# The second layer norm of a gated cross-attention and FFN block: its apply step moved from VectorE to ScalarE

## The chip, the cores and the metric

One core of one Trainium2 chip runs the kernel. The metric is the device time of one execution in microseconds (us). Three runs of the kernel before took 345.74 us in the median (345.51 to 346.2).

## What is computed

```python
# x, ctx: [32, 128, 256]; D = 256; B = 32 sequences, S = 128 positions
x = x + tanh(g_xattn) * mix(layernorm(x), ctx)     # mix: a recurrence over the 128 positions
x = x + tanh(g_ffn)   * ffn(layernorm(x))
# mix, for every position t:
#   r     = decay * r + ctx_t * ctx_t
#   inp   = (ln_t * r) @ Wi.T + bi
#   gate  = sigmoid(inp @ Wg.T + bg)
#   state = tanh((gate * state + (1 - gate) * inp) @ A.T + inp @ Bm.T)
#   out_t = state @ Wo.T + bo
# ffn: relu(ln @ Q(W1).T + b1) @ Q(W2) + b2, with Q a ternary quantisation; F = 1024 hidden units
# layernorm: (x - mean) / sqrt(var + 1e-5), over the last axis, without weights
```

The second layer norm, of x after the attention, is the one that the change concerns.

## The kernel before

The 128 positions are cut into 16 chunks of T = 8 positions. A chunk of x is a tile of 128 partitions by TILES = 2 by 256 values; transposed data has K = 2 blocks of 128 features by N = 256 columns (8 positions of 32 sequences). Products that need more than one pass are written as sums of a high and a low part.

The program is a software pipeline over 18 bodies (`run`, L191 to L198; four are written out at either end and the rest is a loop of two). Body c works on five chunks at once (`stages`, L200): **norm** on chunk c+2, **project** on c+1, **chain** on c, **attend** on c-1 and **ffn** on c-2. So bodies 1 to 16 have an attend stage, bodies 0 to 14 a project stage, bodies 0 to 13 a norm stage, and bodies 0 to 15 a chain stage. Each body has eight slots j = 0 to 7, one for each position of the chain's chunk, and each engine has its own queue, written out by hand slot by slot. An engine does its instructions in that order; semaphores tie the engines together.

The recurrence is the backbone of each slot: VectorE forms m_hi, m_all and m_lo from the last state and the gate (`gated_state`, L573 to L591), TensorE multiplies them (`step`, L840 to L854), ScalarE takes the tanh (`tanh_step`, L427 to L431). Around it stand, in the part of the body that the change touches:

- TensorE: slot 4 `gate_product` (L823), slot 5 the step, three y products and `x1_t` (L868), which transposes xh2 into att_ps; slot 6 the step, two y products and `from_inp(…, 0)` (L828); slot 7 the step, `from_inp(…, 1)` and `from_rest` (L834), which waits for rest_lo.
- ScalarE: slot 5 the tanh, `gate_out` (L390 to L395, two sigmoids of 128x256) and `square` (L365); slot 6 the tanh, `rest_high` (L397) and `normed_high` (L406), the high part of the transposed xh2.
- VectorE: slot 3 `x1_stats` and `x1_mean` (L607, L614) of chunk c-1; slot 5 the gated state, `x1_apply` (L619 to L624) and a hidden low part; slot 6 the gated state, `rest_all` (L561, which waits for the gate), and `scan` (L528 to L541: two small cx instructions and the scan of r for chunk c+2); slot 7 the gated state, `rest_low`, `normed_low` and `finish`.
- GpSimd: once a body, after mean2, the variance plus epsilon (L334) and its power -0.5 (L336) on 128x2 values, then a wait for xh2_set and two accumulating DMAs, of b2_g into x1 (L340) and of bo_g into x_res (L348). The first must not overtake the reading of x1, so it waits until xh2 is written. `finish` (L638) needs b2_added one body later, and `residual` (L599) bo_added in slot 2 of the next body.

Before the bodies and in bodies 0 and 1 TensorE is fed with products of an idle tile (`keep_warm`, L910) wherever it would stand still. All of ScalarE's functions in the bodies (Tanh, Sigmoid, Identity, Relu, Square, copies) run after one table load at the start.

Of the kernel before, what the change touches and what calls it, by code (L numbers as in the profile page):

```python
# [18 lines left out]
def build(nc, x_in, ctx_in, wsq_in, w1_in, w2_in, cols_in, rows_in, out):  # L19
# [33 lines left out]
    with ctx:  # L53
        def sb(name, shape, dt=f32):
            return ctx.enter_context(nc.sbuf_tensor(name, shape, dt))
# [60 lines left out]
        x1 = sb("x1", [P, 2, TILES, D])  # L116
        st2, mv2 = sb("st2", [P, TILES, 6]), sb("mv2", [P, TILES, 2])
        ve2, rs2 = sb("ve2", [P, TILES]), sb("rs2", [P, TILES])
        xh2 = sb("xh2", [P, TILES, D])
        xt_hi = sb("xt_hi", [P, 2, K, N], f16)  # L120
        xt_lo = sb("xt_lo", [P, 2, K, N], f16)
# [38 lines left out]
        bo_added = [sem("bo_added0"), sem("bo_added1")]  # L160
        b2_added = [sem("b2_added0"), sem("b2_added1")]
        stats2, mean2, vare2, rstd2, xh2_set = (sem(n) for n in ("stats2", "mean2", "vare2", "rstd2", "xh2_set"))
        xh2_t, xt_hi_set, xt_lo_set = sem("xh2_t"), sem("xt_hi_set"), sem("xt_lo_set")
        hid_sum, hid_set, h_hi_set, h_lo_set = sem("hid_sum"), sem("hid_set"), sem("h_hi_set"), sem("h_lo_set")
        y_sum, y_set = sem("y_sum"), sem("y_set")
# [112 lines left out]
        def _(pool):  # L278
            nc.gpsimd.memset(idle[:, :], 0.0).then_inc(idle_set, 1)
            nc.gpsimd.memset(ident[:, :], 0.0).then_inc(const_set, 1)  # L280
            nc.gpsimd.memset(ones[:, :], 1.0).then_inc(const_set, 1)
            nc.gpsimd.memset(minus_half[:, :], -0.5)
            nc.gpsimd.memset(eps[:, :], LN_EPS).then_inc(const_set, 1)
            nc.gpsimd.memset(state[:, 1, :, N - B:N], 0.0).then_inc(const_set, 1)
            pool.wait_ge(const_set, 4)
# [34 lines left out]
            def body(c):  # L320
                norm, project, chain, attend, ffn = stages(c)
                if norm:
                    rstd1_of(norm)
                if isinstance(c[0], int) and c[1] == 0:
                    low("wo", wo_scaled, wo_hi, wo_lo)
                    find_below(0, 6)
                if isinstance(c[0], int) and c[1] == 1:
                    find_below(6, 8)
                if attend:

                    if chain:
                        pool.wait_ge(x_res_in[chain[1] % 2], landed(chain))
                    pool.wait_ge(mean2, upto(attend))
                    nc.gpsimd.tensor_tensor(ve2[:, :], mv2[:, :, 1], eps[:, :], ALU.add).then_inc(vare2, 1)  # L334
                    pool.wait_ge(vare2, upto(attend))
                    nc.gpsimd.tensor_tensor(rs2[:, :], ve2[:, :], minus_half[:, :], ALU.pow).then_inc(rstd2, 1)  # L336

                    pool.wait_ge(const_set, 5)
                    pool.wait_ge(xh2_set, upto(attend))
                    pool.dma_start(x1[:, attend[1] % 2, :, :], b2_g[:, :].unsqueeze(1).to_broadcast([P, TILES, D]),  # L340
                                   accum_op=ALU.add).then_inc(b2_added[attend[1] % 2], 16)
                if chain:

                    if isinstance(c[0], int) and c[1] == 0:
                        pool.wait_ge(dve_prep, done["gates_out"])
                    if not attend:
                        pool.wait_ge(x_res_in[chain[1] % 2], landed(chain))
                    pool.dma_start(x_res[:, chain[1] % 2, :, :], bo_g[:, :].unsqueeze(1).to_broadcast([P, TILES, D]),  # L348
                                   accum_op=ALU.add).then_inc(bo_added[chain[1] % 2], 16)
# [4 lines left out]
        def _(act):  # L354
# [53 lines left out]
                nc.scalar.mul(xt_hi[:, q[1] % 2, :, :], att_ps[:, :].rearrange("p (k n) -> p k n", k=K), NORM_SCALE).then_inc(xt_hi_set, 1)  # L408


            def hidden(q, p):
                act.wait_ge(hid_sum, upto(q, PAIRS, p + 1))

                if p >= 2:
                    act.wait_ge(h_lo_set, upto(q, PAIRS, p - 1))
                elif exists(plus(q, -1)):
                    act.wait_ge(h_lo_set, upto(plus(q, -1), PAIRS, PAIRS + p - 1))
                for u in range(2):
                    last = nc.scalar.activation(hid[:, p % 2, u, :], hid_ps[p % 2][:, u * N:(u + 1) * N], ACT.Relu,  # L419
                                                bias=b1_s[:, 2 * p + u:2 * p + u + 1])  # L420
                last.then_inc(hid_set, 1)
# [37 lines left out]
            def body(c):  # L459
# [4 lines left out]
                for j in range(T):  # L464
# [7 lines left out]
                    if j == 3 and project:  # L472
                        inp_out(project)
                    if j == 5:
                        if project:
                            gate_out(project)
                        if norm:
                            square(norm)
# [22 lines left out]
        def _(dve):  # L501
# [114 lines left out]
                    last = nc.vector.bn_aggr(mv2[:, t, :], st2[:, t, :])  # L616
                last.then_inc(mean2, 1)

            def x1_apply(q):  # L619
                dve.wait_ge(rstd2, upto(q))  # L620
                for t in range(TILES):
                    last = nc.vector.tensor_scalar(xh2[:, t, :], x1[:, q[1] % 2, t, :], mv2[:, t, 0:1], rs2[:, t:t + 1],  # L622
                                                   ALU.subtract, ALU.mult)
                last.then_inc(xh2_set, 1)  # L624

            def normed_low(q):
                dve.wait_ge(xt_hi_set, upto(q))
                nc.vector.scalar_tensor_tensor(out=xt_lo[:, q[1] % 2, :, :], in0=att_ps[:, :].rearrange("p (k n) -> p k n", k=K),  # L628
# [102 lines left out]
            def body(c):  # L731
                norm, project, chain, attend, ffn = stages(c)
                peeled = c[1] if isinstance(c[0], int) else None
                for j in range(T):
# [31 lines left out]
                        if ffn:  # L766
                            hidden_low(ffn, 2)
                    if j == 5:
                        if attend:
                            x1_apply(attend)  # L770
                        if ffn:
                            hidden_low(ffn, 3)
                    if j == 6:
# [251 lines left out]
```

## Time and profile before

| | |
|---|---|
| median of three runs | 345.74 us |
| the profiled execution's own time | 345.45 us |
| its span, first to last instruction | 343.7 us |
| TensorE busy | 318.0 us (93%) |
| VectorE busy | 294.7 us (86%) |
| ScalarE busy | 217.0 us (63%) |
| GpSimd busy | 90.8 us (26%) |
| one body, bodies 2 to 13 | 18.47 us |
| mean granted TensorE clock | 0.985 |

The busy times include overlap of an instruction's tail with the next one's start: an instruction's length in a view is from its start to its end, and the next on the same engine can start about 0.1 us before that end. Where the next start is known, the distance of two starts is what an instruction costs its queue. Body c of bodies 2 to 13 begins at about 65.5 + 18.47 (c - 2) us of the span; the body shown in the rows is body 8 (176.8 to 195.3 us). A chain of waits is followed back from the last instruction: it lists, in order of time, the pieces of work of which each released the next.

### The profile page before, as it was taken

The page shows a single profiled execution, that of the slowest core. Times are in us where ns is not written, and L with a number is a line of the kernel's source. Part 1 is how long each engine was busy: PE and PEld are TensorE (multiplying, and loading weights), DVE is VectorE, ACT ScalarE, POOL GpSimd, SP SyncE. Part 2 cuts the span into 40 slices and gives each one's busy share as a digit, 9 for nine tenths or more (in the row PEclk, how much of TensorE's full clock was granted, in tenths as well). Part 3 has the DMA queues.
Part 4 walks back from the last instruction along what each step waited for, and adds up shares of the span by engine and source line. Part 5 has one row for each costly group of instructions (what it writes and reads, how often), then busy time and mean ns, then how long its engine had stood idle before and what let it go on. Part 6 is the DMA issues. An engine that isn't in the chain of part 4 may idle for free.

```text
span 343.7 us, 10093 instructions
## 1 busy us (share of the span) xinstructions
PE 318.0 (93%) x3805; PEld 285.9 (83%) x3805; DVE 294.7 (86%) x868; ACT 217.0 (63%) x501; POOL 90.8 (26%) x119
## 2 busy tenths in 40 slices
PE   8778697899999999999999999999999999999985
PEld 5667586798989898989898998989898989897764
DVE  5885888789989898989898989989898989877653
ACT  3546342486767767675849586766767575847653
POOL 4413951222131312213122222131312212121220
PEclk9989988999999999999999999999999999999999
DMA  7920221614424251716152433324161515150520
GB/s 273 367 96 2 62 32 31 124 33 62 125 42 115 50 137 32 153 31 133 50 94 89 61 122 57 123 34 122 38 145 31 92 31 93 32 93 2 93 62 31
DMA packets 19239, 29.16 MB, mean 85 GB/s; under 512 B 1808, under 2 KB 10000, under 8 KB 18960
## 3 DMA queue, kind: packets, MB, share of 16 engines
q0 software_dynamic: 8704, 8.39, 17.3%
q1 hardware_dynamic: 10080, 19.93, 17.0%
q10 hardware_dynamic: 432, 0.53, 0.5%
q8 instruction: 15, 0.25, 0.3%
q14 instruction: 8, 0.07, 0.1%
HBM read 16.26 MB, written 4.19 MB: 60 GB/s over the span
## 4 chain that ended last, share of the span: by engine, by line
PE 73%; ACT 10%; DVE 10%; issue 3%; POOL 0%; DVEq 0%
PE pre_ps L804 14%; PE hid_ps L890 12%; PE y_ps L902 11%; PE ret_ps L804 8%; PE pre_ps L845 7%; PE inp_ps L804 7%; PE att_ps L863 6%; PE pre_ps L851 4%; ACT inp L384 3%; DVE inp_lo L558 3%; ACT inp_hi L388 3%; PE att_ps L872 2%; PE ret_ps L815 2%; ACT state L429 2%; PE hid_ps L912 1%
## 5 line engine op out<-in xcount | busy, mean ns | idle before, releaser
L429 ACT ACTIVATE state<-pre_ps,sc 128x64 f32<-128x64 f32 x128 | 40.0, 312 | 90.6 <-PE pre_ps L851 90.6
L419 ACT ACTIVATE hid<-hid_ps,b_s 128x256 f32<-128x256 f32 x128 | 53.5, 470 | 13.5 <-PE hid_ps L890 11.8
L890 PE MATMUL hid_ps<-xt_hi,w_q 128*128 128x256 f16 x256 | 59.1, 272 | 1.2 <-DVE xt_lo L628 0.8
L902 PE MATMUL y_ps<-w_q,h_hi 128*128 128x256 bf16 x256 | 59.3, 273 | 0.3 <-DVE h_lo L635 0.3
L890 PE MATMUL hid_ps<-xt_lo,w_q 128*128 128x256 f16 x256 | 59.1, 272 | 0.0
L902 PE MATMUL y_ps<-w_q,h_lo 128*128 128x256 bf16 x256 | 59.1, 272 | 0.0
L635 DVE TENSOR_TENSOR h_lo<-hid,h_hi 128x512 f16<-128x512 f32 x64 | 44.0, 687 | 8.2 <-ACT h_hi L425 6.7
L845 PE MATMUL pre_ps<-m_hi,a_hi 128*128 128x32 f16 x512 | 42.9, 178 | 4.1 <-DVE m_hi L586 3.9
L845 PEld LDWEIGHTS pre_ps<-m_hi,a_hi 128*128 128x128 f16 x512 | 35.1, 96 | 11.0 <-DVE m_hi L586 8.8
L845 PE MATMUL pre_ps<-m_hi,a_lo 128*128 128x32 f16 x512 | 41.8, 176 | 0.0
L425 ACT CAST h_hi<-hid 128x512 f16<-128x512 f32 x64 | 39.6, 619 | 2.0
L586 DVE SCALAR_TENSOR_TENSOR m_hi<-state,gate 128x64 f16<-128x64 f32 x128 | 27.4, 214 | 10.8 <-ACT state L429 10.4
L340 POOL DMA_DIRECT2D x<-b_g x16 | 19.8, 1238 | 56.9 <-DVE xh L622 56.9
L851 PE MATMUL pre_ps<-m_lo,a_hi 128*128 128x32 f16 x512 | 32.5, 177 | 0.6
L845 PEld LDWEIGHTS pre_ps<-m_hi,a_lo 128*128 128x128 f16 x512 | 32.1, 96 | 0.9
L591 DVE TENSOR_TENSOR m_lo<-m_all,m_hi 128x64 f16<-128x64 f32 x128 | 28.8, 225 | 4.4
L334 POOL TENSOR_TENSOR ve<-mv,eps 128x2 f32<-128x2 f32 x16 | 4.5, 282 | 93.7 <-DVE mv L616 93.7
L804 PE MATMUL ret_ps<-inp_hi,wg_hi 128*128 128x256 f32 x64 | 20.1, 314 | 9.1 <-DVE inp_lo L558 9.1
L890 PEld LDWEIGHTS hid_ps<-xt_hi,w_q 128*128 128x128 bf16 x256 | 24.8, 97 | 4.4 <-DVE xt_lo L628 1.1
L902 PEld LDWEIGHTS y_ps<-w_q,h_hi 128*128 128x128 f16 x256 | 24.8, 97 | 4.1 <-DVE h_lo L635 1.0
L588 DVE SCALAR_TENSOR_TENSOR m_all<-state,gate 128x64 f32<-128x64 f32 x128 | 27.8, 217 | 0.0
L902 PEld LDWEIGHTS y_ps<-w_q,h_lo 128*128 128x128 f16 x256 | 25.0, 98 | 2.4
(131 smaller groups left out, 929.1 us busy)
## 6 DMA issues: line engine op xcount, KB each, us to landing
x_norm<-x_in SPq DMA_DIRECT2D x16, 256.0 KB, 2.8
cx<-ctx_in SPq DMA_DIRECT2D x16, 256.0 KB, 3.1
x_res<-x_in SPq DMA_DIRECT2D x16, 256.0 KB, 2.6
x_res<-bo_g POOLq DMA_DIRECT2D x16, 256.0 KB, 4.8
x<-b_g POOLq DMA_DIRECT2D x16, 256.0 KB, 3.9
y_out<-y SPq DMA_DIRECT2D x16, 256.0 KB, 2.0
w_raw<-w_in SPq DMA_DIRECT2D x2, 1024.0 KB, 9.0
wsq<-wsq_in SPq DMA_DIRECT2D x3, 256.0 KB, 6.3
```

Source lines behind the costliest of these rows:

```text
L419: last = nc.scalar.activation(hid[:, p % 2, u, :], hid_ps[p % 2][:, u * N:(u + 1) * N], ACT.Relu, bias=b1_s[:, 2 * p + u:2 * p + u + 1])
L425: nc.scalar.copy(h_hi[:, 2 * p:2 * p + 2, :], hid[:, p % 2, :, :]).then_inc(h_hi_set, 1)
L429: nc.scalar.activation(state[:, q[1] % 2, :, step_cols(j)], pre_ps[q[1] % 2][:, :].rearrange("p (k n) -> p k n", k=K)[:, :, step_cols(j)], ...
L586: nc.vector.scalar_tensor_tensor(out=m_hi[:, :, :], in0=before, scalar=STATE_SCALE, in1=now, op0=ALU.mult, op1=ALU.mult).then_inc(m_hi_set, 1)
L588: nc.vector.scalar_tensor_tensor(out=m_all[:, :, :], in0=before, scalar=STATE_SCALE, in1=now, op0=ALU.mult, op1=ALU.mult).then_inc(m_all_s ...
L591: nc.vector.tensor_tensor(m_lo[:, :, :], m_all[:, :, :], m_hi[:, :, :], ALU.subtract).then_inc(m_lo_set, 1)
L635: nc.vector.tensor_tensor(h_lo[:, 2 * p:2 * p + 2, :], hid[:, p % 2, :, :], h_hi[:, 2 * p:2 * p + 2, :], ALU.subtract).then_inc(h_lo_set, 1)
L804: last = nc.tensor.matmul(out_of(m), w[:, k, cut], v[:, k, :], start=start and n == 0 and (m == 0 or stop), stop=stop and n == len(terms) - 1,
L845: nc.tensor.matmul(pre_ps[q[1] % 2][:, m * N + j * B:m * N + (j + 1) * B], w[:, k, m * P:(m + 1) * P], m_hi[:, k, :], start=False, stop=Fa ...
L851: last = nc.tensor.matmul(pre_ps[q[1] % 2][:, m * N + j * B:m * N + (j + 1) * B], a_hi[:, k, m * P:(m + 1) * P], m_lo[:, k, :], start=Fals ...
L890: last = nc.tensor.matmul(hid_ps[p % 2][:, u * N:(u + 1) * N], w1_q[:, k, cut], v[:, par, k, :], start=n == 0, stop=n == len(terms) - 1)
L902: last = nc.tensor.matmul(y_ps[:, t * D:(t + 1) * D], h[:, f, t * P:(t + 1) * P], w2_q[:, f, :], start=f == 0 and t == 0 and h is h_hi, st ...
```

## The change

Two ScalarE activations, Identity with scale = rs2 and bias = shift2 (both columns of one value per partition), take the place of VectorE's two tensor_scalar instructions. They stand in slot 5 between the tanh and the gate. GpSimd makes the bias, shift2 = -mean2 * rs2, in two instructions more for each chunk, with one semaphore more (scaled2), and a constant of -1 is set once.

```diff
--- before.py
+++ after.py
@@ -116,6 +116,8 @@
         x1 = sb("x1", [P, 2, TILES, D])
         st2, mv2 = sb("st2", [P, TILES, 6]), sb("mv2", [P, TILES, 2])
         ve2, rs2 = sb("ve2", [P, TILES]), sb("rs2", [P, TILES])
+        off2, shift2 = sb("off2", [P, TILES]), sb("shift2", [P, TILES])
+        minus_one = sb("minus_one", [P, TILES])
         xh2 = sb("xh2", [P, TILES, D])
         xt_hi = sb("xt_hi", [P, 2, K, N], f16)
         xt_lo = sb("xt_lo", [P, 2, K, N], f16)
@@ -160,6 +162,7 @@
         bo_added = [sem("bo_added0"), sem("bo_added1")]
         b2_added = [sem("b2_added0"), sem("b2_added1")]
         stats2, mean2, vare2, rstd2, xh2_set = (sem(n) for n in ("stats2", "mean2", "vare2", "rstd2", "xh2_set"))
+        scaled2 = sem("scaled2")
         xh2_t, xt_hi_set, xt_lo_set = sem("xh2_t"), sem("xt_hi_set"), sem("xt_lo_set")
         hid_sum, hid_set, h_hi_set, h_lo_set = sem("hid_sum"), sem("hid_set"), sem("h_hi_set"), sem("h_lo_set")
         y_sum, y_set = sem("y_sum"), sem("y_set")
@@ -280,6 +283,7 @@
             nc.gpsimd.memset(ident[:, :], 0.0).then_inc(const_set, 1)
             nc.gpsimd.memset(ones[:, :], 1.0).then_inc(const_set, 1)
             nc.gpsimd.memset(minus_half[:, :], -0.5)
+            nc.gpsimd.memset(minus_one[:, :], -1.0)
             nc.gpsimd.memset(eps[:, :], LN_EPS).then_inc(const_set, 1)
             nc.gpsimd.memset(state[:, 1, :, N - B:N], 0.0).then_inc(const_set, 1)
             pool.wait_ge(const_set, 4)
@@ -331,9 +335,12 @@
                     if chain:
                         pool.wait_ge(x_res_in[chain[1] % 2], landed(chain))
                     pool.wait_ge(mean2, upto(attend))
-                    nc.gpsimd.tensor_tensor(ve2[:, :], mv2[:, :, 1], eps[:, :], ALU.add).then_inc(vare2, 1)
+                    nc.gpsimd.tensor_tensor(ve2[:, :], mv2[:, :, 1], eps[:, :], ALU.add)
+                    nc.gpsimd.tensor_tensor(off2[:, :], mv2[:, :, 0], minus_one[:, :], ALU.mult).then_inc(vare2, 1)
                     pool.wait_ge(vare2, upto(attend))
-                    nc.gpsimd.tensor_tensor(rs2[:, :], ve2[:, :], minus_half[:, :], ALU.pow).then_inc(rstd2, 1)
+                    nc.gpsimd.tensor_tensor(rs2[:, :], ve2[:, :], minus_half[:, :], ALU.pow).then_inc(scaled2, 1)
+                    pool.wait_ge(scaled2, upto(attend))
+                    nc.gpsimd.tensor_tensor(shift2[:, :], off2[:, :], rs2[:, :], ALU.mult).then_inc(rstd2, 1)
 
                     pool.wait_ge(const_set, 5)
                     pool.wait_ge(xh2_set, upto(attend))
@@ -407,6 +414,13 @@
                 act.wait_ge(xh2_t, upto(q))
                 nc.scalar.mul(xt_hi[:, q[1] % 2, :, :], att_ps[:, :].rearrange("p (k n) -> p k n", k=K), NORM_SCALE).then_inc(xt_hi_set, 1)
 
+
+            def x1_apply(q):
+                act.wait_ge(rstd2, upto(q))
+                for t in range(TILES):
+                    last = nc.scalar.activation(xh2[:, t, :], x1[:, q[1] % 2, t, :], ACT.Identity,
+                                                bias=shift2[:, t:t + 1], scale=rs2[:, t:t + 1])
+                last.then_inc(xh2_set, 1)
 
             def hidden(q, p):
                 act.wait_ge(hid_sum, upto(q, PAIRS, p + 1))
@@ -472,6 +486,8 @@
                     if j == 3 and project:
                         inp_out(project)
                     if j == 5:
+                        if attend:
+                            x1_apply(attend)
                         if project:
                             gate_out(project)
                         if norm:
@@ -615,13 +631,6 @@
                 for t in range(TILES):
                     last = nc.vector.bn_aggr(mv2[:, t, :], st2[:, t, :])
                 last.then_inc(mean2, 1)
-
-            def x1_apply(q):
-                dve.wait_ge(rstd2, upto(q))
-                for t in range(TILES):
-                    last = nc.vector.tensor_scalar(xh2[:, t, :], x1[:, q[1] % 2, t, :], mv2[:, t, 0:1], rs2[:, t:t + 1],
-                                                   ALU.subtract, ALU.mult)
-                last.then_inc(xh2_set, 1)
 
             def normed_low(q):
                 dve.wait_ge(xt_hi_set, upto(q))
@@ -766,8 +775,6 @@
                         if ffn:
                             hidden_low(ffn, 2)
                     if j == 5:
-                        if attend:
-                            x1_apply(attend)
                         if ffn:
                             hidden_low(ffn, 3)
                     if j == 6:
```

## Rows read from the trace of the kernel before

**Rows 1.** Busy time, share and instructions of each engine, from the page
```profile
PE 318.0 (93%) x3805; PEld 285.9 (83%) x3805; DVE 294.7 (86%) x868; ACT 217.0 (63%) x501; POOL 90.8 (26%) x119
```

**Rows 2.** By stretch: length, busy us of PE, PEld, DVE, ACT, POOL; granted clock, DMA
```profile
47.00:65.50 18.50, 15.65 (x182) 13.27 (x182) 14.01 (x42) 7.43 (x19) 8.07 (x8) 0.89 0.30 49
176.80:195.30 18.50, 18.01 (x229) 16.65 (x230) 17.27 (x53) 12.79 (x30) 4.30 (x6) 1.00 0.37 85
324.00:343.70 19.70, 14.69 (x124) 11.30 (x122) 9.47 (x18) 10.49 (x22) 2.51 (x3) 1.00 0.17 41
```

**Rows 3.** TensorE in order of time, steady body (start, length, engine, line, tiles)
```profile
188.57 0.39 PE L804 MATMUL ret_ps<-inp_hi,wg_hi 128*128 128x256 f32 x1 [0.46 <-DVE inp_lo L558]
...
192.16 0.60 PE L872 MATMUL att_ps<-ident,xh 128*128 128x128 f32 x4
...
194.25 0.28 PE L804 MATMUL pre_ps<-inp_lo,bm_hi 128*128 128x256 f32 x1
194.37 0.28 PE L804 MATMUL pre_ps<-inp_hi,bm_lo 128*128 128x256 f32 x1
194.62 0.19 PE L845 MATMUL pre_ps<-m_hi,a_hi 128*128 128x32 f16 x1
```

**Rows 4.** VectorE in order of time, the same body
```profile
191.85 0.22 DVE L591 TENSOR_TENSOR m_lo<-m_all,m_hi 128x64 f16<-128x64 f32 x1
192.12 0.69 DVE L563 SCALAR_TENSOR_TENSOR rest<-gate,inp 128x512 f32<-128x512 f32 x1
...
193.22 1.22 DVE L538 TENSOR_TENSOR_SCAN r<-keep,cx 128x512 f32<-128x512 f32 x1
194.36 0.20 DVE L586 SCALAR_TENSOR_TENSOR m_hi<-state,gate 128x64 f16<-128x64 f32 x1
```

**Rows 5.** ScalarE in order of time, the same body
```profile
191.04 0.31 ACT L429 ACTIVATE state<-pre_ps,sc 128x64 f32<-128x64 f32 x1 [1.20 <-PE pre_ps L851]
191.25 0.83 ACT L393 ACTIVATE gate<-ret_ps,cols 128x256 f32<-128x256 f32 x2
191.97 0.64 ACT L369 ACTIVATE cx<-cx 128x512 f32<-128x512 f32 x1
```

**Rows 6.** The chain of waits in body 1, up to the last step product
```profile
61.44 0.84 ACT gate L393 x2
...
62.30 0.69 DVE rest L563
...
63.41 1.22 DVE r L538
```

**Rows 7.** Groups of ScalarE instructions by line and shape: busy us, mean ns
```profile
L393 ACT ACTIVATE gate<-ret_ps,cols 128x256 f32<-128x256 f32 x32 | 13.3, 471 | 1.4 <-PE ret_ps L804 1.4
...
L404 ACT ACTIVATE s_hi<-state 128x512 f16<-128x512 f32 x16 | 10.1, 630 | 0.8
...
L408 ACT ACTIVATE xt_hi<-att_ps 128x512 f16<-128x512 f32 x16 | 9.6, 597 | 1.5 <-PE att_ps L872 1.5
...
L444 ACT ACTIVATE bm_hi<-wsq,sc 128x512 fp32r<-128x512 f32 x1 | 0.7, 718 | 0.0
```

**Rows 8.** VectorE in order of time, body 14
```profile
304.35 0.22 DVE L586 SCALAR_TENSOR_TENSOR m_hi<-state,gate 128x64 f16<-128x64 f32 x1 [0.62 <-ACT state L429]
```

**Rows 9.** ScalarE in order of time, slot 5 of body 15
```profile
317.64 0.31 ACT L429 ACTIVATE state<-pre_ps,sc 128x64 f32<-128x64 f32 x1
```

**Rows 10.** TensorE in order of time, body 15
```profile
318.48 0.60 PE L872 MATMUL att_ps<-ident,xh 128*128 128x128 f32 x4
```

**Rows 11.** The chain of waits in body 16
```profile
327.48 0.56 POOL ve L334
...
328.10 0.72 POOL rs L336
...
328.85 0.75 DVE xh L622 x2
```

**Rows 12.** GpSimd in order of time, the steady body
```profile
192.30 1.69 POOL L348 DMA_DIRECT2D x_res<-bo_g  x1
```

## The prediction

> **What bounds the kernel now.** I read the page's busy times first. TensorE is busy for 93% of the span, VectorE for 86%, ScalarE for 63% [rows 1]. In a steady body the same holds more sharply: of 18.50 us TensorE is busy for 18.01 and VectorE for 17.27, at a granted clock of 1.00 [rows 2]. By these shares alone an instruction taken from VectorE and given to ScalarE looks like a gain. So the second reading is of one body in order of time, and the question is what TensorE waits for. It waits in two places. Ahead of the gate product it stands still for 0.46 us for inp_lo [rows 3], which hangs on the tanh of slot 3 and lies before the edit. And ahead of the step of slot 7: the last two products of from_inp start at 194.25 and 194.37, 0.12 apart, and the step at 194.62, 0.25 later [rows 3]. So TensorE loses about 0.13 us there, and m_hi of slot 7 (L586) is written at 194.36 + 0.20 = 194.56, just before it starts [rows 4].
>
> Now what puts m_hi there: the third reading, backwards along VectorE and ScalarE. The rest (L563) starts at 192.12, the scan at 193.22 (with the cx pair between them), m_hi at 194.36, each right behind the other [rows 4]. The rest waits for the gate, and the gate pair on ScalarE runs from 191.25 to 192.08, right behind the tanh of slot 5, for which ScalarE had been waiting 1.20 us [rows 5]. VectorE's own m_lo of slot 6 ends at 192.07 [rows 4], the same moment, so this body leaves open which of the two holds the rest. Body 1 decides: there the chain goes from the gate (61.44 + 0.84 = 62.28) to the rest at 62.30 and through the scan of 63.41 [rows 6]. So there is a path with no slack: step 5, tanh, gate, rest, cx, scan, m_hi of slot 7, step 7. The edit puts its two new activations into it, between tanh and gate.
>
> **The cost of the two activations.** The trace has no activation with two columns from SBUF, so I build it. The gate instruction has one column, 256 values and PSUM as its source: 471 ns. A second column costs 718 - 630 = 88 ns (512 values from SBUF, with a column as scale against a constant). SBUF in place of PSUM costs 630 - 597 = 33 ns [rows 7]. Together 471 + 88 + 33 = 592 ns. What counts for the gate behind them is the distance of starts: the gate pair holds the queue from 191.25 to 191.97, 0.36 us for an instruction of 0.47 [rows 5], so 0.11 is overlap. That gives 0.48 with the SBUF term and 0.45 without, as I don't know if that term lengthens the distance or only the tail. I take 0.47, so D = 0.94 us for the pair. The bounds: 0.72 if the second column is free, and 0.98 if nothing of its length is hidden better than in the gate pair. The Trainium skill ("ScalarE: Activation LUTs", section "What ACT_TABLE_LOAD costs") gives 186 ns + 0.833 ns for each value + about 93 ns for each column, with an overlap of about 93: an estimate of 585 ns and a distance of 0.49. That agrees with the 592 built from rows, and by it D is 0.98 and the whole 0.5 us longer than my sum.
>
> **Bodies 1 to 13.** Here attend, project and norm all exist. The gate, the rest, the cx pair, the scan and m_hi of slot 7 all come D later, and TensorE, which has 0.13 us of stall there already and no slack, comes D later with them. Nothing returns it: what follows is from_inp, from_rest and the next body's products, a queue of TensorE at 18.01 of 18.50. The rest_lo that from_rest wants moves with the same D, behind the same m_lo. The transposes x1_t started at 192.16 [rows 3]; xh2 will be ready at 191.25 + 0.47 + 0.59 = 192.31 plus 0.04 for the semaphore, so they come 0.2 later, as does step 6 behind them. That lies inside the D and isn't counted twice. The square and the tanh of slot 6 slip on ScalarE too, to 191.97 + 0.94 + (0.64 - 0.11) = 193.44 [rows 5], while m_hi of slot 7 waits for the scan until 195.3: hidden. Thirteen bodies times 0.94 is 12.2 us.
>
> **Body 14** has no norm stage, so no scan between the rest and m_hi; m_hi of slot 7 had stood 0.62 us waiting for the tanh of slot 6 [rows 8]. The later gate is hidden, and only the 0.2 of the transposes stays. **Body 15** has no gate. The tanh of slot 5 is at 317.64 [rows 9]; xh2 comes at 317.64 + 0.21 + 0.47 + 0.59 + 0.04 = 318.95 against transposes at 318.48 [rows 10]: 0.5. **Body 16** has nothing beside the second norm; the chain is GpSimd ve, rs, then xh2 [rows 11]. The added negation stands ahead of rs; back to back with ve I put 0.2 on it. The last multiplication waits for rs: 0.3, about ve's share of the step from 327.48 to 328.10 without its slow start (bounds 0.2 and 0.62). The pair takes 0.47 + 0.59 = 1.06 where VectorE's took 0.75 [rows 11]: 0.3. Sum 0.8.
>
> **What goes free.** VectorE loses 0.75 us of work a body [rows 11]. It stood in slot 5 ahead of a hidden low part and the m_hi of slot 6, and that m_hi was followed by TensorE's step 6 only behind the transposes; what comes free turns into waiting for the gate. I cost it at nothing, and at most 0.13 us a body (the present stall) if it counted. In the steady bodies GpSimd's two additions run in slot 3 and 4, about 4 us before they are needed. Its DMAs wait for xh2_set and move some 0.9 us later: b2_g is wanted a body later, and x_res<-bo_g, issued at 192.30 [rows 12], only in slot 2 of the next body: hidden. SyncE's loads wait on stages before slot 5 or one body back, so nothing moves there.
>
> The sum: 12.2 + 0.2 + 0.5 + 0.8 = 13.7 us. Against the profiled execution (345.45, of which the span is 343.7 and 1.75 lies around it) that is 359.15; the median of runs is 0.29 above it, 359.4. About 0.2% is what a measurement of this kernel can tell from no change.
>
> **Rivals.**
> 1. *The second column is free, or the pair overlaps better.* D = 0.72: 9.4 for thirteen bodies, 0 in body 14, 0.3 in body 15, 0.6 at the end. 10.3 us, 356.0. For it: only the lack of a row with two columns. Chance 0.12.
> 2. *The gate's delay is absorbed*, because VectorE comes to slot 6 earlier and the rest was really held by VectorE's queue. Then only bodies 14 to 16 lose: 1.5 us, 347.2. For it: m_lo ended within 0.01 us of the gate. Against it: the gate can't start before ScalarE is free, so the delay is real whatever VectorE does. Chance 0.05.
> 3. *VectorE is the bound* (the other side). VectorE's queue is full for 17.27 of 18.50 us [rows 2], and if its last idle is only semaphore time, each body from 1 to 15 gets shorter by what the pair held the queue, about 0.65 of its 0.75 us: 9.7 less, plus 0.8 at the end: 336.8. It decides if rest, in the new trace, still starts right behind m_lo of slot 6 with no waiting for the gate. Against it: TensorE's order has only the 0.13 us stall to give back. Chance 0.03.
> 4. *TensorE's clock falls.* It now stands still for about 1.1 us before step 7. In bodies 0 and 1, where it stands still often, the clock was 0.89, but in the last 19.7 us, busy for 14.69, it was 1.00 [rows 2]. If body 1 goes down to 0.8 that is 18.5 x 0.09 = 1.7 us more, 361.1; if each of 14 bodies ran at 0.98 in place of 1.00, 14 x 18.5 x 0.02 = 5 us more, 364.5. Chance 0.08.
> 5. *The change doesn't run as described*, say a table load around each Identity. The inp activation (L384) is an Identity among the same functions without one; chance 0.01, well over 370.
>
> **How the numbers follow.** The forecast has 0.71. Its own bounds are 356 (D 0.72) to 360.4 (D 0.98, dearer GpSimd ends). The range takes in rival 1 and the mild form of 4: 355.5 to 361.5. Only rivals 2 and 3 aren't clearly slower, and rival 2 is still slower by 0.4%: faster 0.03, same 0.02, slower 0.95.
>
> **What would show it.** In a steady body of the changed kernel: two Identity instructions of about 0.59 us between the tanh of slot 5 and the gate, starts 0.47 apart; VectorE idle for 0.8 to 0.9 us before the rest, released by the gate; TensorE idle for about 1 us before the step of slot 7, released by m_hi; a body of 19.4 us; ScalarE busy for about 14 us of it. If TensorE's wait before step 7 doesn't grow, the path isn't the one I took. If the body grows by more than D, it is the clock or the transposes.

## The result, and the profile after

The changed kernel took 361.18 us in the median of four runs (360.86 to 361.36), the kernel before 345.97 us in its four (345.51 to 348.69): a ratio of 1.044 (1.039 to 1.049), so 15.2 us slower where 13.7 were forecast. The profiled execution took 360.86 us, with a span of 358.7 us, 15.0 longer than before.

First the page's busy times [as rows 1], and the changed kernel's body 8 as a stretch [as rows 2]; its columns are the length and the busy us of TensorE, its weight loads, VectorE, ScalarE and GpSimd, the granted clock, the DMA share and GB/s.

```profile
PE 321.3 (90%) x3805; PEld 285.2 (80%) x3805; DVE 285.4 (80%) x836; ACT 232.9 (65%) x533; POOL 104.0 (29%) x152
```

```profile
183.40:202.90 19.50, 18.28 (x231) 16.62 (x230) 16.75 (x51) 13.76 (x32) 5.12 (x8) 1.00 0.36 81
```

VectorE has lost work and ScalarE has gained it, as the diff says. TensorE's busy time is 3.3 us greater in all, but its share has fallen from 93 to 90%: it waits more. Next, ScalarE in order of time in body 8 [as rows 5]; the columns are start, length, engine, line and tiles, and in brackets the idle time before and who ended it.

```profile
197.69 0.32 ACT L443 ACTIVATE state<-pre_ps,sc 128x64 f32<-128x64 f32 x1 [1.21 <-PE pre_ps L858]
197.90 1.08 ACT L421 ACTIVATE xh<-x,shift,rs 128x256 f32<-128x256 f32 x2
198.88 0.82 ACT L400 ACTIVATE gate<-ret_ps,cols 128x256 f32<-128x256 f32 x2
199.59 0.63 ACT L376 ACTIVATE cx<-cx 128x512 f32<-128x512 f32 x1
```

The pair starts 0.21 us behind the tanh, and the gate 0.98 us behind the pair. VectorE and TensorE in the same body [as rows 4 and 3]:

```profile
198.43 0.23 DVE L607 TENSOR_TENSOR m_lo<-m_all,m_hi 128x64 f16<-128x64 f32 x1
199.74 0.69 DVE L579 SCALAR_TENSOR_TENSOR rest<-gate,inp 128x512 f32<-128x512 f32 x1 [1.08 <-ACT gate L400]
...
200.84 1.23 DVE L554 TENSOR_TENSOR_SCAN r<-keep,cx 128x512 f32<-128x512 f32 x1
201.98 0.20 DVE L602 SCALAR_TENSOR_TENSOR m_hi<-state,gate 128x64 f16<-128x64 f32 x1
```

```profile
199.03 0.66 PE L879 MATMUL att_ps<-ident,xh 128*128 128x128 f32 x4
...
202.24 0.19 PE L852 MATMUL pre_ps<-m_hi,a_hi 128*128 128x32 f16 x1 [0.66 <-DVE m_hi L602]
...
202.63 0.26 PE L858 MATMUL pre_ps<-m_lo,a_hi 128*128 128x32 f16 x4
```

VectorE goes from its own last low part (m_lo, 198.43) into a wait of 1.08 us that the gate ends. From there rest, scan and m_hi follow as before, and TensorE's step of slot 7 waits 0.66 us for m_hi. (That step now starts 18.80 us into the body, 202.24 - 183.44, and started 17.82 us into it before; 0.29 of these 0.98 us already stand ahead of from_inp, because the transposes wait for the pair.) A body (distance of the first from_inp product behind step 7 in two successive bodies, mean of bodies 3 to 13) takes 19.46 us where it took 18.48.

The end, in the chain of waits (start, length, what) [as rows 11]:

```profile
330.76 0.99 ACT xh L421 x2
...
332.29 0.78 POOL x L347
333.08 5.78 DMA x_res<-bo_g
...
338.88 0.76 DVE x L619
...
341.93 0.16 POOL off L339
...
342.16 0.72 POOL rs L341
...
342.95 0.57 POOL shift L343
...
343.54 1.10 ACT xh L421 x2
```

Two things differ from the rows of before. Behind GpSimd's two additions (off at 341.93, shift at 342.95) ScalarE's pair is 1.10 us long. And in body 15 the chain runs through a DMA: the later xh2 holds back GpSimd's issue of b2_g and, behind it in the same queue, of bo_g, and the residual of chunk 15 (DVE x) starts only when that has landed. Measured from the first from_inp products behind step 7 of body 14 (305.87 before, 318.66 after), that issue comes at 14.42 us in place of 13.12.

Laid out by stretches of the two profiled spans, all by the chain of waits:

| stretch | before, us | after, us | difference | forecast |
|---|---|---|---|---|
| to the last products of body 1 | 65.46 | 66.21 | 0.75 | 0.94 |
| bodies 2 to 13 | 222.25 | 234.00 | 11.75 | 11.28 |
| body 14 | 18.16 | 18.45 | 0.29 | 0.2 |
| body 15, to the residual of chunk 15 | 19.09 | 20.22 | 1.13 | 0.5 |
| from there to the end | 18.74 | 19.82 | 1.08 | 0.8 |
| sum | 343.7 | 358.7 | 15.0 | 13.7 |

Single executions far above the rest of their kernel (one each of versions 2, 7 and 9 below, at 362.66, 387.01 and 746.27 us, and two of the kernel before, at 491.78 and 1568.03) are left out of the medians and ratios.

### The profile page after: what moved, and what is told of

It is laid out like the page before. It is cut to its first block, busy times and chain, and to the rows that moved or that the text cites. A ratio compares the mean times of both kernels' runs of the same rounds, so it can differ in the third digit from the quotient of the medians.

```text
span 358.7 us, 10126 instructions
## 1 busy us (share of the span) xinstructions
PE 321.3 (90%) x3805; PEld 285.2 (80%) x3805; DVE 285.4 (80%) x836; ACT 232.9 (65%) x533; POOL 104.0 (29%) x152
## 4 chain that ended last, share of the span: by engine, by line
PE 55%; ACT 18%; DVE 15%; issue 6%; DMA 2%; POOL 1%; ACTq 0%; DVEq 0%; POOLq 0%
PE hid_ps L897 11%; PE pre_ps L811 10%; PE ret_ps L811 7%; PE inp_ps L811 7%; PE pre_ps L852 6%; PE att_ps L870 5%; ACT xh L421 5%; PE pre_ps L858 3%; ACT inp L391 3%; DVE inp_lo L574 3%; ACT gate L400 3%; DVE rest L579 3%; ACT inp_hi L395 3%; PE y_ps L909 2%; ACT state L443 2%
## 5 line engine op out<-in xcount | busy, mean ns | idle before, releaser
L852 PEld LDWEIGHTS pre_ps<-m_hi,a_hi 128*128 128x128 f16 x512 | 35.0, 96 | 18.8 <-DVE m_hi L602 16.7
```

What stands on the lines that cost most here:

```text
L852: nc.tensor.matmul(pre_ps[q[1] % 2][:, m * N + j * B:m * N + (j + 1) * B], w[:, k, m * P:(m + 1) * P], m_hi[:, k, :], start=False, stop=Fa ...
```

## The experiments

Executions of one kernel differ in their granted clock: for the kernel before, means of 0.975 to 0.990 go with times of 348.2 to 343.7 us. In the profiles the clock is below 1.00 only in the first 66 us (90 in version 2), so this lies in the prologue and the first bodies. Medians carry about 2 us of it, and what each experiment did to the body and to the end is read from its profiled execution. "Body" is the mean of bodies 3 to 13 (18.48 before, 19.46 changed); "end" is from the last from_inp products of body 14 to the end of the span (37.83 and 40.04 us). In the code cuts the comments at the right of a line are mine.

| version | median, us | ratio to before (95%) | body, us | end, us |
|---|---|---|---|---|
| changed | 361.18 | 1.044 (1.039 to 1.049) | 19.46 | 40.04 |
| 1 pair in slot 4 | 349.45 | 1.011 (1.005 to 1.017) | 18.48 | 39.51 |
| 2 before, an extra pair | 358.42 | 1.035 (1.028 to 1.041) | 19.48 | 37.79 |
| 3 one column | 357.90 | 1.034 (1.028 to 1.040) | 19.28 | 39.74 |
| 4 GpSimd's additions alone | 347.19 | 1.002 (0.999 to 1.006) | 18.48 | 38.27 |
| 5 bo_g first | 361.77 | 1.046 (1.040 to 1.052) | 19.47 | 39.56 |
| 6 pair behind the gate | 348.76 | 1.013 (1.005 to 1.020) | 18.52 | 39.77 |
| 7 pair in slot 4, scan in slot 5 | 347.07 | 1.003 (1.000 to 1.007) | 18.70 | 38.35 |
| 8 as 7, VectorE normalises | 352.24 | 1.020 (1.014 to 1.025) | 19.12 | 37.83 |
| 9 pair in slot 4, ends mended | 345.88 | 1.001 (0.998 to 1.004) | 18.48 | 38.33 |
| 10 as 7, first norm late | 340.33 | 0.982 (0.979 to 0.985) | 18.17 | 38.37 |
| 11 as 10, VectorE normalises | 341.90 | 0.988 (0.984 to 0.993) | 18.47 | 37.82 |
| 12 as 10, VectorE in body 15 | 339.08 | 0.981 (0.978 to 0.985) | 18.17 | 37.80 |

### Where the pair stands (1, 2, 3, 6)

**1. The pair in slot 4**

```diff
+                    if j == 4 and attend:
+                        x1_apply(attend)
                     if j == 5:
-                        if attend:
-                            x1_apply(attend)
```

> The changed kernel with the two Identity activations moved from slot 5 (between the tanh and the gate) to the end of slot 4 (ahead of the tanh of slot 5), where ScalarE stood idle for 1.2 us in the kernel before. If the loss is the gate's delay on the path tanh, gate, rest, scan, m_hi of slot 7, it goes away: a steady body of 18.35 to 18.5 us, the gate right behind the tanh, and only the end (GpSimd's two additions and the longer pair, about 1.1 us) stays: 346 to 347.5 us. If the loss is ScalarE's greater share of work wherever it stands, the body stays at 19.4 and the time at 360. If VectorE's freed 0.65 us a body is worth something once the gate is on time, about 337 to 340.

ScalarE in a steady body of it:

```profile
187.77 1.09 ACT L421 ACTIVATE xh<-x,shift,rs 128x256 f32<-128x256 f32 x2
189.07 0.32 ACT L443 ACTIVATE state<-pre_ps,sc 128x64 f32<-128x64 f32 x1 [0.21 <-PE pre_ps L858]
189.29 0.83 ACT L400 ACTIVATE gate<-ret_ps,cols 128x256 f32<-128x256 f32 x2
```

The same two instructions stand in the idle time ahead of the tanh of slot 5 (0.21 us of it are left), the gate is right behind the tanh again, and the body is back at 18.48 us. The steady loss is the place, not the work. The median of 349.45 lies above the 346 to 347.5 expected, and 3.6 us above the 345.87 of the kernel before beside it: 1.7 us of that is the end (39.51 against 37.83, where I had put 1.1), and the rest goes with the clock. The execution with a mean of 0.989 took 345.56 and those with 0.974 took 349.5 to 349.7, where the kernel before took 343.7 to 345.2 at 0.990 and 346.5 to 348.0 at 0.975. VectorE's row is telling too: its 0.65 us are free here and the gate on time, and the body isn't shorter than before.

**2. An extra pair in the kernel before**

```diff
+            def extra_pair():
+                for t in range(TILES):
+                    nc.scalar.activation(spare[:, t, :], w_abs[:, t, 0:D], ACT.Identity,
+                                         bias=cols[:, C_BI:C_BI + 1], scale=cols[:, C_DECAY:C_DECAY + 1])
...
                     if j == 5:
+                        if attend:
+                            extra_pair()
                         if project:
                             gate_out(project)
```

> The kernel before, VectorE's normalisation untouched, with two Identity activations of the same shape with two columns, on other data into a spare tile, ahead of the gate in each body with an attend stage. If the gate's delay is the whole steady loss and VectorE's freed time is worth nothing, a body takes 19.47 us as in the changed kernel, and the time is 346 + 13 x 1.0 + 0.2 = 359.1 us. If VectorE's freed time gave something back in the changed kernel, the body here is longer than there by that much: up to 19.6 us (361) if the 0.13 us stall counted, and 20.1 us (367) if it is VectorE's queue.

```profile
241.18 1.09 ACT L414 ACTIVATE spare<-w_abs,cols 128x256 f32<-128x256 f32 x2
242.16 0.82 ACT L394 ACTIVATE gate<-ret_ps,cols 128x256 f32<-128x256 f32 x2
```

0.98 us again, and a body of 19.48, with VectorE's work untouched. The changed kernel's body is 0.02 us shorter than this: VectorE's freed 0.65 us were worth no more than that in it. (The profiled execution of this version took 362.66 us, at a mean clock of 0.971; from body 3 on its clock is 1.00 and every body takes 19.47 to 19.49 us.)

**3. One column**

```diff
                     last = nc.scalar.activation(xh2[:, t, :], x1[:, q[1] % 2, t, :], ACT.Identity,
-                                                bias=shift2[:, t:t + 1], scale=rs2[:, t:t + 1])
+                                                scale=rs2[:, t:t + 1])
```

> The changed kernel with the bias column left out of the two activations (the norm then lacks its mean). If the distance of starts is what counts and a column costs 0.09 us of it, the pair holds the queue for 0.80 in place of 0.98 us, a body takes 19.29 us, and the time is 361.2 - 13 x 0.18 - 0.2 = 358.6 us. If the second column only lengthens the tail, the pair's distance and the time stay as they are: 361.

This version leaves out the subtraction of the mean.

```profile
197.86 0.89 ACT L421 ACTIVATE xh<-x,rs 128x256 f32<-128x256 f32 x2
198.66 0.82 ACT L400 ACTIVATE gate<-ret_ps,cols 128x256 f32<-128x256 f32 x2
```

The pair now holds the queue for 0.80 us: 0.09 for a column and instruction, all of it in the distance of starts. The body is 0.18 shorter, the same 0.18 that the pair lost. Nothing between the pair and TensorE takes up any of it.

**6. The pair behind the gate and the square, transposes behind slot 6's y products**

```diff
                         if norm:
                             square(norm)
+                        if attend:
+                            x1_apply(attend)
...
-                    if j == 5 and attend:
+                    if j == 6 and attend:
                         x1_t(attend)
```

> The changed kernel with the two activations behind the gate and the square in slot 5, and the transposes of xh2 behind the y products of slot 6. ScalarE has exactly the same instructions. If only the gate's delay counts, a body takes 18.48 us and the time is 347 to 348 us, the end as in the changed kernel. If the later xh2, or the tanh of slot 6 that now stands behind the pair, takes its place, a body takes 18.8 to 19.5 us.

```profile
191.80 0.83 ACT L400 ACTIVATE gate<-ret_ps,cols 128x256 f32<-128x256 f32 x2
...
193.03 1.09 ACT L421 ACTIVATE xh<-x,shift,rs 128x256 f32<-128x256 f32 x2
194.02 0.31 ACT L443 ACTIVATE state<-pre_ps,sc 128x64 f32<-128x64 f32 x1
```

The gate is on time. The tanh of slot 6 is late (194.02, right behind the pair), but m_hi of slot 7 stands behind the scan and is written at 195.11, ahead of its step at 195.39. What sets the pace is another wait. The chain of waits of this body runs from the pair into the transposes:

```profile
193.15 0.98 ACT xh L421 x2
...
194.18 0.66 PE att_ps L879 x4
```

The last y product ahead of them starts at 193.77, and such products follow each other every 0.11 us, so TensorE loses 0.3 us there; step 7 then takes 0.31 us and has no stall left (0.63 us in the kernel before). One wait has taken the place of the other, and the body is 18.52, 0.04 over that of before. So two quite different places with the gate on time both remove the loss of 0.98 us, and no cause but the gate's delay is left for it.

### The ends (4, 5, 9)

**4. GpSimd's additions in the kernel before**

```diff
-                    nc.gpsimd.tensor_tensor(ve2[:, :], mv2[:, :, 1], eps[:, :], ALU.add).then_inc(vare2, 1)
+                    nc.gpsimd.tensor_tensor(ve2[:, :], mv2[:, :, 1], eps[:, :], ALU.add)
+                    nc.gpsimd.tensor_tensor(off2[:, :], mv2[:, :, 0], minus_one[:, :], ALU.mult).then_inc(vare2, 1)
...
-                    nc.gpsimd.tensor_tensor(rs2[:, :], ve2[:, :], minus_half[:, :], ALU.pow).then_inc(rstd2, 1)
+                    nc.gpsimd.tensor_tensor(rs2[:, :], ve2[:, :], minus_half[:, :], ALU.pow).then_inc(scaled2, 1)
+                    pool.wait_ge(scaled2, upto(attend))
+                    nc.gpsimd.tensor_tensor(shift2[:, :], off2[:, :], rs2[:, :], ALU.mult).then_inc(rstd2, 1)
```

> The kernel before with GpSimd's two additions alone; VectorE still normalises and waits until both are done. If they are hidden in the steady bodies and bare only in body 16, the body stays at 18.47 us and the time grows by 0.16 + 0.6 = 0.8 us to 346.7. If GpSimd's operations hold up VectorE's where the two meet, a body grows by 0.05 us or more and the time passes 347.5.

```profile
327.48 0.55 POOL ve L338
328.02 0.16 POOL off L339
...
328.25 0.72 POOL rs L341
...
329.04 0.20 POOL shift L343
```

The body doesn't move, so the additions are hidden there. At the end off takes 0.16 us, shift 0.20 and the gap ahead of it 0.07, and the end is 0.44 us longer, not 0.8: shift lasts 0.20 here against 0.57 in the changed kernel. VectorE stands idle meanwhile here; in the changed kernel it does a hidden low part at that moment.

```profile
342.76 0.69 DVE L644 TENSOR_TENSOR h_lo<-hid,h_hi 128x512 f16<-128x512 f32 x1 [0.88 <-ACT h_hi L439]
```

```profile
342.95 0.56 POOL L343 TENSOR_TENSOR shift<-off,rs 128x2 f32<-128x2 f32 x1
```

The multiplication starts 0.19 us into that instruction and ends at 343.51, 0.06 behind its end. In the steady bodies of the changed kernel it is the same: shift took 676 ns in the median, 194 at the least, and in body 8 it ran (194.53 to 195.21) beside inp_lo (194.46 to 195.15).

**5. The bo_g DMA ahead of the wait for xh2**, in the changed kernel

```diff
+                    if chain:
+                        pool.dma_start(x_res[:, chain[1] % 2, :, :], bo_g[:, :].unsqueeze(1).to_broadcast([P, TILES, D]),
+                                       accum_op=ALU.add).then_inc(bo_added[chain[1] % 2], 16)
                     pool.wait_ge(const_set, 5)
                     pool.wait_ge(xh2_set, upto(attend))
...
-                if chain:
+                if chain and not attend:
```

> The changed kernel with the bo_g DMA issued ahead of GpSimd's wait for xh2, in place of behind it. In the steady bodies that DMA is hidden either way: a body stays at 19.46 us. In body 15 of the changed kernel the residual waits for it (the chain of waits ends in a DMA of 5.78 us); issued earlier it falls off the chain and the stretch from the last from_inp products of body 14 to the end (40.0 us in the changed kernel) is 0.5 to 0.8 us shorter: about 360.5. If the residual waited for TensorE anyway, that stretch stays.

```profile
332.04 0.99 ACT xh L424 x2
...
333.07 0.66 PE att_ps L882 x4
...
338.84 0.67 PE att_ps L873 x6
...
339.62 0.76 DVE x L622
```

The DMA is off the chain: the residual now follows TensorE's output product (338.84 + 0.67). The end is 0.48 us shorter (39.56 against 40.04), just under the 0.5 to 0.8 that I gave. What is left of body 15's loss, 19.68 against 19.09 us to the residual, is the wait of the transposes for the pair (332.04 to 333.03). The median of 361.77 doesn't show the half us under the clock's spread.

**9. The pair in slot 4, bo_g first, and VectorE normalising in body 16**

```diff
+                    if j == 4 and attend and chain:        # ScalarE
+                        x1_apply(attend)
...
+                        if attend and not chain:           # VectorE, slot 5
+                            x1_apply(attend)
```

GpSimd's two additions are left out in body 16 as well.

> The activations in slot 4 as in the first experiment (18.48 us a body there), the bo_g DMA ahead of the wait for xh2, and VectorE's normalisation without GpSimd's additions in body 16. If the DMA and the longer GpSimd and ScalarE chain are all that is left at the end, the stretch from the last from_inp products of body 14 to the end is 37.8 us, as in the kernel before (39.5 in the first experiment), and the time that of the kernel before within 0.3%. If something else of the change costs there, it stays 0.5 us or more longer.

The time is that of before (1.001, 0.998 to 1.004). The end is 38.33 us, 0.5 over the 37.8 expected, so something else of the change does cost there; experiment 12 shows what.

### What VectorE's freed time can be used for (7, 8, 10, 11, 12)

**7. The square ahead of the pair in slot 4, the scan in slot 5**, on top of 9

```diff
+                    if j == 4 and norm:                    # ScalarE
+                        square(norm)
...
-                        if norm:                           # ScalarE, slot 5
-                            square(norm)
...
+                        if norm:                           # VectorE, slot 5, behind hidden_low(ffn, 3)
+                            scan(norm)
...
-                        if norm:                           # VectorE, slot 6
-                            scan(norm)
```

> A version meant to use what VectorE gains. The activations in slot 4, the square of the norm stage ahead of them in slot 4, and the cx pair and scan on VectorE in slot 5 behind the hidden low part, where the normalisation stood, so that neither lies between the gate and m_hi of slot 7. The bo_g DMA is issued ahead of the wait for xh2, and in body 16 VectorE normalises without GpSimd's additions. If VectorE's freed time has value once the scan fills it, TensorE's 0.13 us stall ahead of step 7 goes, a body takes 18.35 us, and the time is 1.6 us under the kernel before: 344.3. If m_hi of slot 6 behind the scan comes too late for step 6, a body takes 18.5 or more and the time is that of before or above.

**8. The same move with VectorE normalising** (the kernel before as base)

> The kernel before with the same move of the square to slot 4 and of the cx pair and scan to slot 5, but with VectorE still normalising in slot 5. VectorE then has 0.65 us more ahead of m_hi of slot 6 than in the version with the activations on ScalarE. If the freed time is what makes the move possible, m_hi of slot 6 comes about 0.5 us too late for step 6: a body of 18.8 to 19.0 us and a time of 350 to 352 us. If VectorE's time has no value here, a body of 18.35 us and 344.2.

VectorE in version 7:

```profile
188.62 0.69 DVE L582 TENSOR_TENSOR inp_lo<-inp,inp_hi 128x512 fp32r<-128x512 f32 x1 [0.70 <-ACT inp_hi L403]
189.23 0.97 DVE L548 TENSOR_SCALAR xh<-x_norm,mv,rs 128x256 f32<-128x256 f32 x2
...
190.72 0.21 DVE L610 SCALAR_TENSOR_TENSOR m_hi<-state,gate 128x64 f16<-128x64 f32 x1
...
192.34 1.23 DVE L562 TENSOR_TENSOR_SCAN r<-keep,cx 128x512 f32<-128x512 f32 x1
193.48 0.20 DVE L610 SCALAR_TENSOR_TENSOR m_hi<-state,gate 128x64 f16<-128x64 f32 x1
```

Both missed the gain, and 8 is 0.12 us a body over the 18.8 to 19.0 that I expected of it. The scan is off the gate's path, but now m_hi of slot 6 (193.48) is late for step 6, and in both the chain of waits runs along VectorE's queue from inp_lo to that m_hi. In 8, with the normalisation in the same queue, the body is 0.41 us longer than in 7. But the two differ in one thing more: 7 issues the bo_g DMA ahead of the wait for xh2, 8 behind it. In 7 the two first-norm instructions (L548) take 0.97 us in place of 0.73; they run beside that issue:

```profile
188.69 0.68 POOL L344 TENSOR_TENSOR shift<-off,rs 128x2 f32<-128x2 f32 x1
189.31 1.23 POOL L351 DMA_DIRECT2D x_res<-bo_g  x1
```

In 8 the same pair takes 0.73 us (191.15 to 191.88). With these 0.24 us the sum closes. Behind m_lo of slot 5 the chain of waits needs 1.33 us to the cx pair in 8 (192.93 to 194.26, the normalisation and the low part) and 0.69 in 7 (191.24 to 191.93, the low part alone): 0.64 more, less the 0.24, is 0.40, against the 0.41 between the bodies. So once the path lies in VectorE's queue, its freed time counts in full. How long 7 takes with the DMA left in its old place wasn't run.

**10. The first norm's apply step moved from slot 4 to slot 6**, on top of 7

```diff
-                        if norm:                           # VectorE, slot 4
-                            norm_apply(norm)
...
                         if project:
                             rest_all(project)
+                        if norm:                           # VectorE, slot 6
+                            norm_apply(norm)
```

> The version with the scan in slot 5, and besides the first norm's apply step (L524 of the kernel before, 0.65 us of VectorE) moved from slot 4 to slot 6 behind the rest, where VectorE stood idle. In the version before it, the scan held m_hi of slot 6 until 0.2 us a body too late (a body of 18.70 us). The scan now starts about 0.6 us earlier. If VectorE's queue ahead of that m_hi was the cause, TensorE's stalls ahead of steps 6 and 7 go and a body takes 18.35 us, 0.13 under the kernel before: 12 bodies bring 1.6 us, 344.4. If the square or the hidden high part of slot 4 on ScalarE holds the scan, the body stays above 18.48.

**11. The same order with VectorE normalising**

> The same order as the version with the scan in slot 5 and the late first norm, but with VectorE doing the second normalisation in slot 5. The two differ only in who normalises. VectorE has 0.65 us more ahead of m_hi of slot 6: I expect a body of 18.55 to 18.75 us here against 18.35 there, so 346.5 to 349 us. If both take the same, VectorE's freed time has no value in this order either.

The chain of waits in a steady body of 10:

```profile
188.64 0.19 PE pre_ps L869 x8
...
188.93 0.88 PE y_ps L926 x8
189.81 0.71 PE pre_ps L828 x6
190.52 0.21 PE pre_ps L869 x8
190.73 0.10 PE pre_ps L875 x4
190.83 2.25 PE pre_ps L828 x18
```

Between the gate product and the end of the body it is TensorE alone, and step 7 takes 0.21 + 0.10 us. The body is 18.17, which is what body 14 of the kernel before took, the one body that has a gate but no scan. I had expected 18.35. In 11 the body is 18.47, under the 18.55 to 18.75 expected: the order alone brings next to nothing there, as the normalisation now holds the gated state of slot 6, and step 6 takes 0.60 us in the chain of waits in place of 0.29. Between 10 and 11 lie 0.30 us a body. They differ in who normalises in bodies 1 to 15 and, with it, in GpSimd's two additions and the place of the bo_g DMA; neither stands on the chain of waits of a steady body. The 0.30 is less than the 0.65 of work, and it is all that TensorE had to give back. Version 10 takes 340.33 us, 0.982 of before. Its twelve steady bodies account for 12 x 0.32 = 3.8 of the 6.4 us, and its end gives 0.5 back. The rest lies ahead of body 2, whose start comes at 63.2 us in its profile against 65.5 in the kernel before and 64.6 in version 9; the order differs there too, and so does the clock, and the two weren't separated. Version 11 is under the kernel before by 1.2% with nearly the same body, so its gain lies in that first stretch too (60.7 us in its profile, at a clock of 1.00 throughout), with the same two causes open.

**12. VectorE normalising in body 15 too**, on top of 10 (`project` in place of `chain` in the three conditions)

> The fastest order so far (scan in slot 5, late first norm), with VectorE normalising in body 15 as well, where ScalarE's pair stands right ahead of the tanh of slot 5 and the step products have nothing to hide it. The stretch from the last from_inp products of body 14 to the end was 37.8 us in the kernel before and 38.4 with the pair on ScalarE in body 15. If the pair is what costs there, the stretch is 37.8 again and the time about 0.5 us less, 339.8 against 340.3. If not, it stays at 38.4.

The end is 37.80 us, that of the kernel before, and the time 339.08 us (0.981, 0.978 to 0.985), where I expected 339.8. So the half us of 9 and 10 was the second norm of body 15 on ScalarE. This version drops its pair and GpSimd's two additions there together; the chain of waits of 9 names the pair: it runs through it (316.86, 1.00 us) into the transposes at 317.91, and the tanh of slot 5 stands behind it. In 9 that tanh comes 12.79 us after the start of the body's first from_inp products (304.97), where it came 11.77 after in the kernel before (305.87 and 317.64 [rows 9]):

```profile
316.77 1.09 ACT L429 ACTIVATE xh<-x,shift,rs 128x256 f32<-128x256 f32 x2
317.76 0.29 ACT L451 ACTIVATE state<-pre_ps,sc 128x64 f32<-128x64 f32 x1
```

## Why the prediction was right

**The path.** Right, and shown from both sides: the pair ahead of the gate costs the body 0.98 to 1.00 us with VectorE relieved (changed) or not (2), and nothing when it stands elsewhere (1, 6). VectorE waits for the gate (1.08 us, forecast 0.8 to 0.9) and TensorE for m_hi (0.66 us, forecast about 1; 0.29 of the delay stands ahead of from_inp instead).

**The range.** The measured 361.18 us lies above my own bounds for this path (356 to 360.4). It is inside the stated range, up to 361.5, by the room that I had kept for a falling clock, and the clock didn't fall: in the changed kernel's profile it is 0.86 from 44 to 66 us (0.84 before) and 1.00 from there on. That the number came out inside is in part luck: what filled that room are the misses that follow. And the 0.2% that I took as the least difference that can be told is too little: single executions of the kernel before span 343.7 to 348.7 us.

**The size of D.** The instruction was 588 ns long (592 built from rows). The distance of starts was 0.49, not 0.47: D is 0.98, the upper bound that I gave. The estimate by the figures of the Trainium skill ("ScalarE: Activation LUTs", "What ACT_TABLE_LOAD costs") was a distance of 0.49, and the trace agrees. Halving the SBUF term between distance and tail was the step that was off: with the whole of it my own rows gave 0.48, and the last 0.01 is an overlap of 0.10 in place of 0.11. No run sets an SBUF and a PSUM source side by side in this instruction, so where that term lies isn't shown by itself. Times twelve bodies this is 0.5 us of the 1.3 us that were missing.

**Body 15** was the step that failed: "x_res<-bo_g ... only in slot 2 of the next body: hidden". That holds in a full body. Bodies 15 and 16 are short of work, and there the DMA that GpSimd issues behind the later xh2 reached the residual. It cost 0.5 us (5); the transposes cost 0.6, where I had put 0.5 on body 15. The trace of before had the evidence: the bo_g DMA of body 15 is issued at 318.99 and lands 4.8 us later, and the residual starts at 324.96, which leaves 1.2 us of room. In the changed kernel the issue comes 1.3 us later and the DMA takes 5.8. I had looked at a steady body only.

**The end.** From ve to rs it is 0.15 us longer and from rs to the pair 0.63, where I had 0.2 and 0.3: shift was mis-sized (0.57 us beside VectorE's low part, 0.20 without it in 4). The pair was 1.10 for 1.06.

**The stall ahead of step 7** was mis-sized, though the sum didn't hang on it: I read 0.13 us from the start of the step and took that as all that could come back. The step waits twice, for m_hi and for m_lo behind it. In the chain of body 8 of before it lasted until 195.28 from 194.65, 0.63 us, against 0.31 in version 10. The difference is the 0.32 us by which that version's body is shorter.

**VectorE is the bound** (rival 3) was wrong for this order of work: in 1 and 9 its time is free and nothing comes back. **The gate's delay is absorbed** (rival 2) fell with 3. **The clock** (rival 4) stayed at 1.00 in bodies 2 to 13. **A free second column** (rival 1) fell with 3.

## What to carry to other kernels

A shift of work from an engine at 86% to one at 63% is judged by the place in the receiving queue: two activations in 1.2 us of idle time ahead of a tanh cost the body nothing, and the same two 1.5 us later, behind that tanh and ahead of the gate, cost their whole 0.98 us in each body. What the giving engine gains is worth nothing until something on the path is moved into the gap; then it was worth 0.30 us a body here, all that the bound engine had still been waiting. And what is hidden in the steady bodies has to be looked up again in the last two, where the cover is thin.

## What the runs showed of the hardware

- A small two-input operation of GpSimd that starts while VectorE does a 128x512 instruction with two SBUF inputs ends right behind it. In the changed kernel shift2 on 128x2 values took 194 ns in body 15, where no such instruction ran, and 420 to 715 in bodies 2 to 14 and 16, where it ended 0.05 to 0.06 us behind inp_lo or a hidden low part each time. The trace of before has it too: ve in body 16 took 0.56 us beside a low part, 0.24 in body 15. A power was lengthened as well in body 15 of the changed kernel, where it started 0.07 us behind a low part (rs2, 1187 ns against 689), and not in body 15 of before, where it started 0.05 us ahead of one (0.72 us). The Trainium skill ("GPSIMD Engine Reference", "1. Specifications") says that GpSimd's interfaces to SBUF are shared with VectorE, with contention with instructions that have two SBUF inputs; these rows agree with it and add the size. That this sharing is the cause was not tested by itself.
- In the other direction VectorE's first normalisation of 128x256 values took 0.97 us for the pair beside GpSimd's issue of a DMA (7), and 0.73 without (8, and the changed kernel).
- A column operand costs an activation 0.09 us, in its distance to the next and not only in its tail (0.98 and 0.80 us for a pair).
